# Preparing a batch inside the attention of the batch ahead, in a transformer block with sixteen-head attention and a mixture of experts

## The reference

```python
coeff = softmax(coeff_weight[x], axis=-1)                # [4, 1024, 4]: 4 numbers per token id
bases = base_embed_weight + lang_bias                    # [4, 256]
h = einsum('bsn,nd->bsd', coeff, bases) * 16.0 + lang_bias[2] * 0.1

def attn(x):                                             # x = layernorm(h), 16 heads of 16
    p = einsum('bsd,ed->bse', x, Wv) + bv                # q = k = v = p
    scores = einsum('bhqd,bhkd->bhqk', q, k) / 4.0
    out = einsum('bhqk,bhkd->bhqd', softmax(scores), v)
    return einsum('bsd,ed->bse', out, Wo) + bo
h = h + attn(layernorm(h))

def moe(x):                                              # x = layernorm(h), 8 experts, top 2
    top, idx = top_k(x @ router, 2); w = softmax(top)
    return sum over the two experts e of w_e * ((silu(x @ w1[e]) * (x @ w3[e])) @ w2[e])
return h + moe(layernorm(h))
```

## Time and profile before

| | us |
|---|---|
| median of 3 runs | 965.76 |
| profiled execution, its own time | 964.48 |
| its span, first to last instruction | 962.7 |
| busy: TensorE / VectorE / ScalarE / GpSimd | 795.8 / 503.1 / 553.7 / 374.8 |
| first exponential of the attention | 93.22 |
| exponentials, 342 of them, busy | 466.9 |
| mean granted TensorE clock | 0.928 |

### The profile page before, as it was taken

How to read it: one execution, slowest core, us unless ns; L and a number is a source line. 1 busy time by engine, 2 the same in 40 slices (tenths; PEclk the granted TensorE clock), 3 DMA queues, 4 the chain that set the end, 5 groups by cost and what they waited for, 6 DMA issues and landing times. The chain is left out here.

```text
span 962.7 us, 17366 instructions
## 1 busy us (share of the span) xinstructions
PE 795.8 (83%) x5581; PEld 346.4 (36%) x5582; DVE 503.1 (52%) x1513; ACT 553.7 (58%) x518; POOL 374.8 (39%) x314
## 2 busy tenths in 40 slices
PE   4053988898999889988998898219999999999994
PEld 2042322222222222222222222106666666666662
DVE  5076034656465655647555566735555555555552
ACT  0032698988999999999999998002222222222221
POOL 6782200211242022221222115624656666656552
PEclk9565799999999999999999999559999999999998
DMA  1000101031201111011110123224454545544541
GB/s 25 2 1 20 44 2 34 12 34 45 65 13 44 35 44 45 13 56 45 45 40 17 34 66 89 66 55 76 86 96 82 96 85 96 90 91 84 92 70 23
DMA packets 71613, 49.52 MB, mean 51 GB/s; under 512 B 45279, under 2 KB 67441, under 8 KB 71554
## 3 DMA queue, kind: packets, MB, share of 16 engines
q1 hardware_dynamic: 55298, 31.22, 13.6%
q0 software_dynamic: 16256, 17.55, 11.0%
HBM read 22.79 MB, written 17.56 MB: 42 GB/s over the span
## 5 line engine op out<-in xcount | busy, mean ns | idle before, releaser
L889 ACT ACTIVATE shared<-PS 128x1536 f32<-128x1536 f32 x342 | 466.9, 1478 | 38.7 <-PE PS L692 37.3
L702 PE MATMUL PS<-shared,va 128*32 128x512 f32 x2048 | 276.2, 612 | 5.1 <-DVE acc_s L1127 4.7
L846 POOL DMA_INDIRECT slots<-pair_no,pos_i x64 | 63.2, 988 | 373.9 <-DVE pos_i L1014 359.2
L1256 PE MATMUL PS<-w_p,xsT 128*128 x828 | 191.8, 382 | 11.7 <-DMA xsT<-xs 11.6
L692 PE MATMUL PS<-qf,ak 32*128 32x512 bf16 x1024 | 131.1, 389 | 42.2 <-ACT shared L889 38.0
L1225 POOL DMA_INDIRECT out<-y_s,idx_tok x68 | 107.5, 1581 | 83.0 <-ACT y_s L1310 70.6
L1305 ACT ACTIVATE act_s<-PS 128x512 f32<-128x512 f32 x69 | 41.2, 597 | 162.4 <-PE PS L1256 162.4
L1256 PEld LDWEIGHTS PS<-w_p,xsT 128*128 128x128 f16 x828 | 81.2, 98 | 98.3 <-issue 17.0
L1358 DVE CAST hidT<-PS 128x512 bf16<-128x512 f32 x68 | 47.0, 691 | 126.8 <-PE PS L1265 126.8
L1273 PE MATMUL PS<-shared,hidT 128*128 x828 | 102.9, 275 | 3.7 <-issue 3.7
L692 PEld LDWEIGHTS PS<-qf,ak 32*128 32x128 bf16 x1024 | 31.6, 91 | 206.3 <-ACT shared L889 156.0
(11 more groups left out here) (270 smaller groups left out, 700.4 us busy)
## 6 DMA issues: line engine op xcount, KB each, us to landing
w_raw<-w SPq DMA_DIRECT2D x24, 512.0 KB, 4.6
xrows<-rows SPq DMA_DIRECT2D x16, 258.0 KB, 3.1
out<-h1s SPq DMA_DIRECT2D x16, 256.0 KB
xs<-xrows,idx_tok POOLq DMA_INDIRECT x70, 2.9
xsT<-xs SPq DMA_TRANSPOSE x70, 3.6
out<-y_s,idx_tok POOLq DMA_INDIRECT x68, 4.1
slots<-pair_no,pos_i POOLq DMA_INDIRECT x64, 6.0
cw<-coeff,xi POOLq DMA_INDIRECT x32, 2.3
```

The source lines that it names most:

```text
L702: last = pe.matmul(PS[32 * slot:32 * slot + 32, ACC, :], g.va[:, KT * (grp // HG) + kt, c, :], prob[:, (4 * quad + slot) % (RING * WIDE), ...
L846: pool.indirect_dma_start(g.slots, bass.IndirectOffsetOnAxis(pos_i[:, grp % 2, 2 * k + kk:2 * k + kk + 1].bitcast(U32), 0), g.pair_no[:, t ...
L889: act.activation(prob[:, at:at + n, :].rearrange("p n q -> p (n q)"), PS[:, buf:buf + n, :].rearrange("p c q -> p (c q)"), ACT.Exp).then_i ...
L1256: last = pe.matmul(PS[:, up_bank(k) + half, :], xsT[:, k, 2 * a + c, :], g.w13_p[:, w, c, ds(e, 1), FF * half:FF * half + FF].rearrange("p ...
```

## The change

Stages one, two and four become one program, `attention`, without a meeting of the engines between them; row maxima become a second pass.

- Gathers are counted batch by batch. GpSimd issues those of batches 0 and 1, copies batch 0's values, then those of 2 and 3, then the constants that only the later part of the attention wants. The ones with an early use are made by VectorE (identity, head mask, fills of `va` and `xq`).
- The preparation of a batch is one set of functions for 8 tiles: `tokens_shifted`, the exponential on ScalarE, `tokens_varied`, `tokens_normal` (three Newton steps on VectorE, no table), `tokens_split`, `turn_tokens`, `turn_keys`. For batch 0 it stands ahead of the attention. For batch b it is spread over groups 4(b-1) to 4(b-1)+3, with TensorE's pieces after quads 12 and 15.
- The own score is a form in the products of the 5 numbers (25 columns more in `xtok`), so one product of 2 x 512 columns for a batch replaces 8 of the 32 small ones. The shift is one of the batch, of one bfloat16 part; the keys `krb` have two buffers for it.
- All eight pair products stand in group 0, after quads 4 to 7 and 11 to 14. The rank product stands after quad 14, not 13.
- The last `places_out` but one stands behind the last accumulator copy. GpSimd does three splits, not four, ahead of the last positions. The accumulator's copy adds 1e-30.
- The flag is worked out in group 12. The experts run in any case; after them, if the flag is set, come the row maxima, the attention and the experts once more. Most scratch tiles are carved out of the room that the first experts' weights and one common tile take.

```diff
-            pool.wait_ge(x_in, 16)
-            for t in range(NT):
-                pool.indirect_dma_start(g.cw[:, t, :], None, ins["coeff"],
-                                        bass.IndirectOffsetOnAxis(g.xi[:, t:t + 1].bitcast(U32), 0)).then_inc(gathered, 16)
...
-            pool.wait_ge(gathered, 16 * NT)
...
-            link(dve.tensor_reduce(tmax[:], g.cw[:], X, ALU.max))
...
+            pool.wait_ge(x_in, 16)
+            gather(0)
+            gather(1)
+            pool.wait_ge(va_zeroed, 1)
+            values(0)
+            gather(2)
+            gather(3)
+            constants()
...
+        def tokens_shifted(batch):
+            cw = g.cw[:, KT * batch:KT * batch + KT]
+            dve.wait_ge(gathered[batch], 16 * KT)
+            link(dve.tensor_reduce(tmax[:], cw, X, ALU.max))
...
+        if initial:
+            weights_and_keys()
+            turn_tokens(0, 0, 0)
+            turn_tokens(0, 1, 1)
+            turn_keys(0, 2)
+            pe.wait_ge(kq_in, 16 * NA)
+            pe.wait_ge(kr_copied, 1)
+            own_scores(0, 4)
...
+    def preparing(grp, step):
+
+        batch = grp // HG + 1
+        return batch if initial and grp % HG == step and batch < NBATCH else None
...
-                if quad in (5, 6):
-                    pair_product(quad - 5)
-                if 1 <= grp < HG and at in (11, 12):
-                    pair_product(2 * grp + at - 11)
...
+                if at in (4, 5, 6, 7):
+                    pair_product(at - 4)
+                if at in (11, 12, 13, 14):
+                    pair_product(at - 7)
...
+            if at == 12 and preparing(grp, 1):
+                pe.wait_ge(u_read, 2 * grp + 4)
+                turn_tokens(preparing(grp, 1), 0, UB)
+            if at == 12 and preparing(grp, 2):
+                pe.wait_ge(u_read, 2 * grp + 4)
+                turn_keys(preparing(grp, 2), UB)
...
+            if at == 15 and preparing(grp, 1):
+                pe.wait_ge(rank_read, grp)
+                turn_tokens(preparing(grp, 1), 1, UB)
+            if at == 15 and preparing(grp, 2):
+                pe.wait_ge(rank_read, grp)
+                own_scores(preparing(grp, 2), UB)
...
-            for n in range(BESIDE, BESIDE + WB + 1):
-                low(n)
-            note(GROUPS - 1)
+        for n in range(BESIDE, BESIDE + WB):
+            low(n)
+        note(GROUPS - 1)
...
+            needed = eng.value_load(g.flag[0:1, 0:1], min_val=0, max_val=1)
+            run(eng)
+            with eng.If(needed > 0):
```

2167 lines of the change are left out of this document (1141 added, 1026 removed).

## The result

| us | before | after |
|---|---|---|
| median (4 runs each, one chip) | 966.38 | 920.21 |
| lowest to highest | 964.62 to 967.29 | 919.41 to 921.18 |
| profiled execution, its span | 962.7 | 918.3 |
| first exponential | 93.22 | 37.85 |
| first to last exponential | 503.3 | 515.8 |

The ratio is 0.9525, with a 95% interval of [0.9507, 0.9542]: 46 us faster, where I forecast 53.8 and a range of 902 to 920. The time lies 0.2 us outside it.

A forecast was written before the change was run, and what follows sets the result against it. ScalarE's exponentials were taken as the bound from 93.22 to 596.5 us, after a start needing only batch 0's tokens, with TensorE bounding the experts. Terms summed to −52.7 from 964.48, giving 911.8, forecast as 912 us, range 902 to 920.

The forecast's parts named there:

- batches 2 and 3 prepared, groups 4 to 15: Inside attention, the part of the +5 us for preparing batches 1 to 3 that falls in these groups: +3.3 us.
- experts and ends: Experts' loop unchanged; second pass's skip moves to the end and each engine reads the flag: +0.5 us, at most +2.
- The start: Before attention: only batch 0's eight gathers and tokens come first, first exponential at 36.9 us: −56.3 us (−60 to −50).
- The clock term: Group 0: TensorE's clock low from about 22 to 63, 26 us of attention at half clock against 17.5: +4.2 us.
- The products: Group 0: six more pair products, each costing 0.7 us because TensorE is nearly full: +4.2 us.
- Groups 1 to 3: These attention groups lose their six pair products, and ScalarE idles less: −7.3 us (−8 to −5).
- the other batches inside attention: Batches 1 to 3 prepared during attention: twelve TensorE pieces at 0.35 us and three exponentials at 0.3: +5 us (0 to +14).
- Rival (b): Attention: each of twelve preparation pieces costs near 1.16 us, 13.9 in place of 4.2, giving 922 us; chance 0.12.
- The tail: Between attention and experts: positions and table come sooner, VectorE's chain ends at about 630.5, not 633.5: −3 us (−5 to 0).
- The criterion: Forecast wrong if attention's exponentials take over 516 or under 498 us, or the first starts after 42.
- Rival (a): Early attention: clock rises early, full from about 47 us, giving 904 us; chance 0.15.
- rival (c): Start: VectorE's chain is 6 us longer, by holds against GpSimd or waits on key transfers, giving 918 us; chance 0.14.

The follow-up runs named there:

- e3_all_gathers: Changed kernel, with all 32 token gathers issued and awaited before batch 0's tokens: 950.83 us, ratio 0.9737 to the kernel before.
- e7_pe_shifted: Changed kernel plus 40 products of 16 columns on TensorE in the start: ratio 0.9572 to the kernel before, executions between 920.96 and 932.3 us.
- e8_four_pairs: Changed kernel without the second four of group 0's eight pair products: first 34 exponentials took 60.25 us, against 63.6 in the changed kernel.
- e4: Changed kernel without preparing batches 1 to 3, which read batch 0's data: attention 506.5 us, 12.4 less than e1_again.
- e1_again: The changed kernel once more, unedited, on another set's chip: 928.8 us, ratio 0.9501 to the kernel before.
- e10: Changed kernel, with SyncE waiting for the end of group 2 ahead of all it does for group 1: 917.19 us, one execution.
- e15: Changed kernel with kr_rows declared behind slots, so slots lies behind xrows in memory, no instruction changed: ratio 0.9348 to the kernel before.
- e18: Changed kernel with kr_rows declared 64 KB long instead of 10 KB, still ahead of slots: 916.76 us, ratio 0.9423 to the kernel before.

## Why the prediction missed by 8

| step | forecast | measured |
|---|---|---|
| first exponential | −56.3 | −55.4 |
| group 0: products and clock | +8.4 | +4.1 |
| groups 1 to 3 without products, batch 1 prepared | −5.6 | +5.5, of it 8.8 the stop |
| batches 2 and 3 prepared, groups 4 to 15 | +3.3 | +2.7 |
| tail | −3 | 0 |
| experts and ends | +0.5 | −1.4 |
| span | −52.7 | −44.4 |

**The start** was right, and by its own steps: tokens at 15.55 for 15.9, fills ended at 27.9 for 26.6, first exponential 37.85 for 36.9. VectorE had no gap of 1 us from 16 to 32.

**Group 0.** The clock term was wrong: I took the low stretch to have a fixed length of 41 us. It ended 16.9 us after the first exponential, as before (17.3), and e3_all_gathers, where attention began 29 us later and the clock rose 17 us after that, shows that its end goes with the attention. So +4.2 was 0. In no profile was the full clock back sooner than 14.9 us after the first exponential (e7_pe_shifted), and in the profile after it stood at half until 54.8 though TensorE worked without a gap from 42.1 on. What the trace records is the granted share, 0.50; the 1.2 GHz beside it in my forecast agrees with an estimate from the profile before: a score product of 512 columns took 0.603 us at half clock and 0.384 at full (L692, medians of 95 to 110 and of 113 to 134), so if the 0.219 us between them are half of what 512 columns take at half clock, that clock moves 1.17 columns per ns. The products were sized about right: 0.7 us each forecast; the first row after is 4.1 us longer with six more of them, so 0.7 each if nothing else changed there (5.3 us over the first 34 exponentials, 0.9 each), and e8_four_pairs gives 0.6 to 1.05.

**Groups 1 to 3.** The products' leaving and batch 1's work came to −3.3 without the stop; −5.6 forecast. **This is the step that failed in size: "the other batches inside attention" and what surrounds it held no term for a stop of the whole core: nothing in the sum, 8.8 us measured.** What opens it stays open, as said above. The time without it would be 911.4, against 912. That closeness is luck in part: the clock's +4.2 that did not come paid for the tail's −3 and for the rest here. And 912 was itself 1.3 too low for its own sum: 52.7 off the median of 965.76 is 913.1.

**The preparation** cost 1.9 (batch 1, e4's second stretch against after, stops taken off), 2.3 and 1.3 us, 5.5 in all, for the 5 forecast; e1_again beside e4 gives 7. Rival (b), 13.9, is out. But it isn't spread over twelve holes under 0.5 us: 1.72 us is VectorE held by a weight split in group 5.

**The tail.** Positions were written 4.1 us sooner, counted from the last exponential (17.2 against 21.3), and the table was gathered 3.8 us sooner, as forecast. My path was wrong. I had the tail end with VectorE's chain, held by a split, and that hold was under-sized: 2 us by the earlier trace rows, 3.36 and 4.86 measured, the second over two splits back to back. But it cost nothing, as VectorE was done 3.5 us ahead of the experts' first fill. The tail ends with GpSimd, and the step from its last piece to the fill took 9.4 us (585.35 to 594.77) where it had taken 5.9 (631.99 to 637.89):

```profile
637.89 0.92 DVE L1344 MEMSET xs<- 128x1032 f32 x1 [2.79 <-PEq L629]
```

Of the 3.5 us more, the drain at the stage's end took 2.6: it ended 8.0 us after the last piece (593.35), 5.4 before (637.37). From there to the fill it was 0.9 us more (1.42 and 0.52), in which every engine now reads the flag. So the 3.8 us won were given back there. Why the drain is longer is not known.

**The criterion** (over 516 us first to last exponential) was just not met at 515.8, and would have been on e1_again's chip. Rival (a) had its early clock (full from about 47) nowhere (from 52.0 at the earliest, in e7_pe_shifted); rival (c) has the right size (918) but not the mechanism, as VectorE's start chain was 0.9 us longer, not 6.

## What to carry to other kernels

Look for an engine with room in an earlier stage before leaving a later stage's work ahead of it: three batches' tokens cost 5 to 7 us inside the attention, where ScalarE was busy for 116.6 of 123.7 us and VectorE, with them, for 84.0, and taking them out of the start, with the ends of stages around them, gave 26. Splitting a queue of gathers by its first consumer gave 29. When a large gain comes in some us short, look for one hole in which all engines stand at once before pricing the small terms, and look at what the queues did 10 to 20 us earlier (13 to 19 here). GpSimd's splits held a two-column VectorE instruction for 4.86 us (0.16 without them) and the flags' cast for 4.11 (0.19), but ask first which engine the next stage waits for: here it was GpSimd, whose last piece counted and not VectorE's chain.

## What the chip did that I had not expected

- A stop of all engines (in e10 of ScalarE and TensorE only), 4 to 13 us, 13 to 19 us behind a group of scatters of single words. Where that tensor of words lay in device memory made it 3.0 us or none (e15, e18), and the ratio to before 0.935 and 0.942 in place of the 0.950 to 0.953 of other sets.
- Beside it packets of 1032 bytes took up to 9 us (0.05 as a rule), and a 16 KB instruction fetch, where one fell there, 3 to 6 us (1 as a rule).
- The clock's rise, 15 to 19 us after the first exponential, was the same after 65 us at half clock as after 37.
- A two-column vector operation took 4.86 us beside GpSimd's splits, 0.16 without them.
- The experts' first fill came 9.4 us after GpSimd's last piece in all nineteen profiles of the changed kernel and its variants, whatever VectorE did, and 5.9 us in the kernel before.
